# Back-scans read their masked values from the PSUM bank they came from; the convolution's sigmoid goes to PSUM

## What is computed

```
h = relu(layernorm(x));  x = x + gat(h)
h = relu(layernorm(x));  x = x + conv(h)

gat, 4 times:
    fs = (h @ W).reshape(N, H, D)
    e = leaky_relu(el[src_e] + er[dst_e], 0.2)
    alpha = softmax of e over the edges of one destination
    h = (segment_sum(alpha[:, :, None] * fs[src_e], dst_e) + b).sum(axis=1)
conv:
    total = batch_norm(concat(h[src], h[dst], nbr) @ W_full + b_full)
    filter_fea, core_fea = split(total, 2)
    nbr_msg = sigmoid(filter_fea) * softplus(core_fea)
    upd = segment_sum(nbr_msg, dst)
    return softplus(h + batch_norm(upd))
```

## Time and profile before, and how to read it

| | |
|---|---|
| median of 3 runs | 3179.8 us (3177.26, 3179.8, 3186.66) |
| profiled execution, its own time | 3188.4 us |
| its span, first to last instruction | 3186.6 us |
| mean granted clock of TensorE | 0.819 |
| the three spreads' gathers on POOL, first to last start | 818.5 to 2074.5 us, with other steps between them |
| last edge stage's gathers, first to last start | 2320.0 to 2606.7 us |
| conv stage's scatters, first to last start | 2666.1 to 2944.3 us |

### The profile page before, as it was taken

The page is one execution under the profiler, slowest core; times in us unless marked ns, Lnnn a source line. Parts: engine busy times, 40 slices in busy tenths (PEclk is TensorE's granted clock), DMA queues, the critical chain, the costliest instruction groups (busy, mean ns, idle before and its releaser), DMA issues. The chain is left out here.

```text
span 3186.6 us, 38276 instructions
## 1 busy us (share of the span) xinstructions
PE 2305.1 (72%) x10796; PEld 1490.8 (47%) x10796; DVE 2230.3 (70%) x3891; ACT 1248.8 (39%) x2599; POOL 1434.1 (45%) x1389
## 2 busy tenths in 40 slices
PE   1998888399899399898569898749967781110575
PEld 1766665255575255566345565425533330000564
DVE  4766665677776567687377687468889976664698
ACT  0332332144332144343134333124445547662586
POOL 5777775000577300377500177700067754777000
PEclk9999999999855599777589877569989975555898
DMA  2333333011453111254101155202233321222464
GB/s 60 105 102 101 100 96 84 13 47 46 105 125 87 16 37 46 70 143 113 25 23 46 52 133 134 41 20 79 79 74 71 73 55 35 65 72 64 146 199 141
DMA packets 310382, 248.80 MB, mean 78 GB/s; under 512 B 149840, under 2 KB 258639, under 8 KB 310154
## 3 DMA queue, kind: packets, MB, share of 16 engines
q1 hardware_dynamic: 266270, 197.56, 20.6%
q0 software_dynamic: 43904, 48.80, 8.7%
HBM read 125.76 MB, written 118.06 MB: 77 GB/s over the span
## 5 line engine op out<-in xcount | busy, mean ns | idle before, releaser
L933 POOL DMA_INDIRECT edge<-table,row_of_source x588 | 596.9, 1015 | 909.4 <-POOLq L753 731.2
L871 PE MATMUL banks<-scaled_t,w_heads 128*64 128x512 f32 x784 | 380.1, 607 | 0.0
L815 DVE TENSOR_TENSOR_SCAN wide<-keep,wide,banks 64x512 f32<-64x512 uint8 x196 | 249.5, 1273 | 185.9 <-issue 161.3
L1229 POOL DMA_INDIRECT edge<-table,row_of_x x196 | 226.3, 1155 | 305.9 <-POOLq L131 244.6
L849 ACT ACTIVATE ring<-wide 128x512 f32<-128x512 f32 x196 | 123.6, 630 | 425.4 <-DVE wide L815 425.4
L1073 ACT ACTIVATE wide<-h_new 64x512 f32<-64x512 f32 x147 | 92.6, 630 | 474.1 <-DVE h_new L1019 474.1
L981 PEld LDWEIGHTS banks<-w_edge_full,wide 128*128 128x128 f32 x1176 | 219.6, 278 | 122.7 <-issue 105.9
L1488 POOL DMA_INDIRECT node_rows<-rows_conv,scatter_row x196 | 218.9, 1117 | 118.8 <-ACT rows_conv L1526 68.2
L981 PE MATMUL banks<-w_edge_full,wide 128*128 128x72 f32 x1176 | 227.7, 360 | 54.9 <-DVE self_logit L1029 54.0
L878 PEld LDWEIGHTS banks<-w_row,ring 128*128 128x128 f32 x1568 | 190.4, 191 | 161.1 <-issue 149.3
L974 PE MATMUL banks<-wide,w_row 128*64 128x512 f32 x294 | 241.6, 920 | 19.4 <-DVEq L1006 10.1
(11 more groups left out here) (300 smaller groups left out, 4571.9 us busy)
## 6 DMA issues: line engine op xcount, KB each, us to landing
node_rows<-x_out SPq DMA_DIRECT2D x97, 256.0 KB, 2.6
wide<-node_rows SPq DMA_DIRECT2D x48, 512.0 KB, 3.6
table<-chain_rows SPq DMA_DIRECT2D x147, 136.0 KB, 2.2
table<-rows SPq DMA_DIRECT2D x147, 136.0 KB, 2.3
nodes<-in_x_dram SPq DMA_DIRECT2D x97, 128.0 KB, 2.5
table<-x_out SPq DMA_DIRECT2D x97, 128.0 KB, 2.4
out_dram<-n_soft SPq DMA_DIRECT2D x48, 256.0 KB, 2.1
sources<-src_pad SPq DMA_DIRECT2D x49, 196.0 KB
```

What stands on the lines that cost most here:

```text
L815: v.tensor_tensor_scan(out=wide[0:D, bass.ds(g * GE + 1, GE)], data0=keep[:, s], data1=bank[2 + s][0:D], initial=wide[0:D, bass.ds(g * GE, ...
L871: last = t_.matmul(bank[2 + s][0:D], w_heads[:, l, pair], scaled_t[:, s, pair], start=pair == 0, stop=pair == 1)
L933: pool.indirect_dma_start(out=edge[:, at_tile], out_offset=None, in_=tables[l], in_offset=bass.IndirectOffsetOnAxis(ap=row_of_source[:, at ...
L1229: pool.indirect_dma_start(out=edge[:, tile, 0:D], out_offset=None, in_=tables[l], in_offset=bass.IndirectOffsetOnAxis(ap=row_of_x1[:, tile ...
```

## The change

The masking writes its result into the bank that it reads, and the back-scan reads it there, in `spread` and in the last edge stage. PE's next product into that bank therefore waits until the back-scan has read it (`spread_out`), and no longer for the masking (`ended_ready`). The tiles `ended` go. In the conv stage ACT writes the sigmoid into partitions 64 to 127 of bank 4 or 5, DVE multiplies it with the softplus from there, and the product goes to a tile of its own, `gated`, which the scan reads. No instruction is added, removed or moved in any engine's list.

```diff
@@ spread(l)
-                ended = mem(st, f"ended_{l}", [D, 2, GE])
...
                     def weights(k, g, s, turn):
-                        t_.wait_ge(ended_ready, at(k, back=2))
+                        t_.wait_ge(spread_out, at(k, back=2))
                         t_.matmul(bank[s % 2][0:D], w_row[:, l, 0:D], wide[:, bass.ds(g * GE + 1, GE)], start=True, stop=True).then_inc(through, 1)
...
                     def end(k, g, s, turn):
                         v.wait_ge(keep_in[s], turn * 16 + 16)
                         v.wait_ge(through, at(k))
-                        v.scalar_tensor_tensor(out=ended[:, s % 2], in0=keep[:, s % 2], scalar=0.0, in1=bank[s % 2][0:D],
+                        v.scalar_tensor_tensor(out=bank[s % 2][0:D], in0=keep[:, s % 2], scalar=0.0, in1=bank[s % 2][0:D],
                                                op0=ALU.is_equal, op1=ALU.mult).then_inc(ended_ready, 1)
...
-                        v.tensor_tensor_scan(out=h_new[:, s % 2, ::-1], data0=keep[:, s % 2, ::-1], data1=ended[:, s % 2, ::-1],
+                        v.tensor_tensor_scan(out=h_new[:, s % 2, ::-1], data0=keep[:, s % 2, ::-1], data1=bank[s % 2][0:D, ::-1],
                                              initial=h_new[:, 1 - s % 2, 0:1], op0=ALU.mult, op1=ALU.add).then_inc(spread_out, 1)
@@ last edge stage: the same
-            ended = mem(st, "ended_last", [D, 2, GE])
...
-                    t_.wait_ge(ended_ready, at(k, back=2))
+                    t_.wait_ge(spread_out, at(k, back=2))
...
-                    v.scalar_tensor_tensor(out=ended[:, s], in0=keep[:, s], scalar=0.0, in1=bank[s][0:D],
+                    v.scalar_tensor_tensor(out=bank[s][0:D], in0=keep[:, s], scalar=0.0, in1=bank[s][0:D],
...
-                    v.tensor_tensor_scan(out=h_new[:, s, ::-1], data0=keep[:, s, ::-1], data1=ended[:, s, ::-1],
+                    v.tensor_tensor_scan(out=h_new[:, s, ::-1], data0=keep[:, s, ::-1], data1=bank[s][0:D, ::-1],
@@ conv stage
-            gate = mem(st, "gate", [P, 2, GE])
+            gated = mem(st, "gated", [D, 2, GE])
...
-                    s_.activation(gate[D:P, s % 2], soft[0:D, s], ACT.Exp, scale=-1.0).then_inc(gate_ready, 1)
+                    s_.activation(bank[4 + s % 2][D:P], soft[0:D, s], ACT.Exp, scale=-1.0).then_inc(gate_ready, 1)
...
-                    v.tensor_tensor(gate[0:D, s % 2], gate[D:P, s % 2], soft[D:P, s], ALU.mult).then_inc(message_ready, 1)
+                    v.tensor_tensor(gated[:, s % 2], bank[4 + s % 2][D:P], soft[D:P, s], ALU.mult).then_inc(message_ready, 1)
...
-                    v.tensor_tensor_scan(out=wide[0:D, bass.ds(g * GE + 1, GE)], data0=keep[:, s], data1=gate[0:D, s % 2],
+                    v.tensor_tensor_scan(out=wide[0:D, bass.ds(g * GE + 1, GE)], data0=keep[:, s], data1=gated[:, s % 2],
```

## The result

The changed kernel takes 3134.8 us in the median of four runs (3129.66 to 3135.99), the kernel before 3183.2 us beside it (3177.26 to 3193.14): ratio 0.9826, 95% interval 0.9802 to 0.985. That is 48 us less by the two medians and 55 us less by the ratio. The forecast was -39 us, with a range of 3130 to 3164 us counted from 3179.8; against 3179.8 the ratio gives 3124.5 us. Direction and mechanism hold; the saving is larger than the range allows.

What follows compares the result with a forecast made beforehand. No engine was taken to bound the whole kernel: POOL bounds the spreads and conv, DVE the last edge stage. The terms -36 + 0 + 0 - 3 gave -39 us, 3141 us against the median 3179.8, range 3130 to 3164.

Steps and rivals of the forecast that it cites:

- The scan no longer holds a gather, -40.6 us: Spreads: with one scan operand in PSUM, gathers starting inside a back-scan are no longer held; 40.6 us as upper bound.
- I take 36 us saved of the 40.6, with 25 and 41 as ends: Spreads: net saving after some holds come back at the row statistics' subtraction and scaling.
- Those that start near a scan's end lose little, as the last of them shows.: Spreads: of 138 gathers starting during a back-scan, late starters lose little; the one at 2063.22 was the example.
- Some holds come back at L1038 and L1048, 4.7 to 11 us.: Spreads: POOL's starts fall more often into these two-SBUF-operand operations, 4.7 us, plus 6 us where a hit repeats.
- POOL stays the bound.: Spreads: POOL comes out 12 us earlier per spread, against 48 us of DVE waits for gathers, so ends move with POOL.
- PE's product waits for the scan.: Spreads: the moved wait counts only at starts, 1.3 us late in four stages, covered by POOL; 5 us without cover.
- The masking's write to PSUM, 0, between -3 and +26.: Masking in spreads and last edge stage: writing PSUM costs about 5 ns each, taken as 0; bounds 3 us less, 26 more.
- Rival (3): Masking reads and writes one bank at half rate, 0.53 us more each; +23 us, 3203 us in all; chance 0.06.
- Last stage, 0.: Last edge stage: gathers get up to 23 us shorter, but DVE is the bound and gathers are early, so worth 0.
- Conv, -3 us, 2 to 9.: Conv: the product's 18.8 us of holds go, but scatters then meet `larger` or the scan; 2 to 9 us shorter, 3 taken.
- Rival (2): The scan still holds POOL despite one operand in PSUM; 3177 to 3180 us, no change; chance 0.09.
- Rival (1): Another bound appears in the spreads, leaving half their saving: -18 - 3, about 3159 us; chance 0.09.

Runs made afterwards that it cites:

- e4: Kernel before, but the spreads' back-scan writes h_new to PSUM banks 6 and 7, both inputs still in SBUF: 3595.5 us, ratio 1.0011, on the chip of 3593 us.
- e1: Kernel before with only the three spreads' part of the change (masking result left in PSUM): 3612.8 us, ratio 1.005, on the chip of 3593 us.

## Why the prediction was right and where it was wrong

- *The scan no longer holds a gather, -40.6 us.* Right in mechanism (`e4` against `e1`: the second SBUF operand decides) and right for the execution it was read from: 596.9 to 557.3 us. **The step that failed is its size, "I take 36 us saved of the 40.6, with 25 and 41 as ends".** It took one execution's holds for the kernel's upper bound. Three other executions with the spreads of before have 605.5, 607.8 and 611.4 us of gathers, so that 48 to 54 us go, and the spreads alone measured -47 us. This is the larger part of the miss: some -48 where -36 stood.
- *"Those that start near a scan's end lose little, as the last of them shows."* True of those near the end, but the last row is no example: the gather at 2063.22 starts 0.06 us behind the start of its scan, at 2063.16, and loses nothing because the scan waits for it. The prediction did not have this case, and it decides the conv's first steps.
- *Some holds come back at L1038 and L1048, 4.7 to 11 us.* Mis-sized: everything above 0.944 us outside the scans is 2.8 us now and was 2.3 before, so next to nothing comes back.
- *POOL stays the bound.* Right: DVE still waits 99.3 us for gathers in 40 combines, before 143.4. The 44 us are the saving, taken from the cover as the prediction counted it.
- *PE's product waits for the scan.* It waits in 10 places, 17.3 us, not only at the starts, and longer than 1.3 us; POOL covers it. In time that term is 0, as forecast.
- *The masking's write to PSUM, 0, between -3 and +26.* Right: 680 ns against 671 in the spreads, 9 ns a piece, 0.4 us over the last stage. Rival (3), half rate, did not occur. The cycle table of the Trainium skill ("VectorE: DVE Perf Modes") prices a source in PSUM, 62 cycles above one in SBUF, and not a write; the 65 ns that the prediction's estimate made of it are seen neither for the write (9 ns) nor, in the earlier trace rows, for the source (5 ns).
- *Last stage, 0.* Right, though the first comparison of two profiles seemed to refute it with -6.0 us: the stage alone gives 0.9999.
- *Conv, -3 us, 2 to 9.* **Mis-sized: 9 us**, the end of the range. The rhythm of the steady part came out as worked out, with 3.0 us less in its last 32 steps. The second step that failed is "I take 3" out of 2 to 9: it goes by the steady part, and in the first eight steps, where 5.8 us went, DVE's operations follow each other at once, and the product's hold went without a new one, since there the scan waits for the scatter.
- *Sum, -39 us.* With the sizes measured it is -48 + 0 + 0 - 9 = -57 us, against 48 to 55 measured. The low end of 3130 us is 50 us below the median that the prediction started from. It went by the sum of the terms' own bounds, -53, and the largest of these, the 41 us of the spreads, was one execution's.
- *Rival (2), the scan still holds POOL.* Did not occur: `e4` has gathers of 1.81 us beside a scan with two operands in SBUF, the changed kernel 0.94 us beside the other. The section "Who interferes with whom" of the Trainium skill ("SBUF — State Buffer") says that an instruction with two SBUF inputs contends with a GpSimd instruction that reads SBUF, and infers that generating descriptors is not stalled by it. The prediction made of the inference that the change would bring nothing. But a gather has its row numbers in SBUF, so the section's rule can cover its start, and the 128 gathers that were under way when a scan began and took 0.94 us agree with the inference.
- *Rival (1), another bound in the spreads.* Did not occur on the chips of 3190 us. On the others another bound, PE's late results, is there before the change already, and there the change brings a loss: a case that the prediction did not have, since it took one chip's trace for the kernel's.

## What to carry to other kernels

Where POOL issues indirect transfers back to back, look for DVE operations beside it that read two tensors from SBUF, and move one of them into a PSUM bank that is free at that moment, if only by writing a result in place: the write costs 9 ns, and each hold, of up to 1.0 us, comes back in full where POOL is the bound. Measure it on more than one chip: where POOL was not the bound, the same change cost 1.3%. A saving that depends on where two free-running engines meet varies between executions (40.6 to 53.3 us of holds here), so read it from more than one before its size is forecast, and price a pipeline's first steps apart from its steady part. A stage whose length differs between two profiles without a change of its own differed here with the clock of TensorE in its tail; measuring that part of the change alone told the two apart.

## What the runs showed of the hardware

- A gather that starts inside a DVE scan with both data operands in SBUF, from 0.10 us behind its start on, ends 0.75 us behind that scan or takes its full time if that is longer, wherever the scan writes; with one operand in PSUM it takes 0.94 us.
- A gather that is already under way when such a scan starts takes 0.94 us (128 of 128). One that starts in the scan's first hundredths of a microsecond is not held either, and the scan takes up to 1.35 us instead of 1.27.
- The same kernel takes 3190 us on two chips and 3533, 3593 and 3614 us on three others, 11 to 13% more, most of it in the stages with gathers, where PE's results come late (in the spreads by some 4 us in up to every second step); a change worth -1.7% on the one kind costs 1.3% on one of the other.
- ACT writes the sigmoid into PSUM in 585 ns, into SBUF in 628 ns.
